# Orthogonal FFT convolution: the turned copy of U by a VectorE shuffle, and two copies moved from GpSimd to ScalarE

## The chip, the cores and the metric

The kernel runs on one core of a Trainium2 chip. The metric is the device time of one execution in microseconds, as the median over several executions. The profile is of one execution of its own.

## The reference, cut to what matters

```python
def cal_wfft_ortho(weight, n, cout, cin):            # n = 34, weight 128 x 127 x 3 x 3
    vfft = rfft2(weight, s=(n, n), norm='ortho')     # 34 x 18 frequencies
    vH = conj(swapaxes(vfft, -1, -2))
    wfft = vH @ vfft                                  # one 127 x 127 matrix per frequency
    eps = mean(diagonal(wfft)) * 1e-5
    wfft = wfft + eps * eye
    ortho = I - 2.0 * (vfft @ solve(wfft, vH))
    return ortho[:, :, :cout, :cin]

xfft = rfft2(pad(_gn(x)))                             # x: 32 x 128 x 32 x 32, group norm first
zfft = cal_wfft_ortho(weight, ...) @ xfft             # per frequency
out  = x + crop(irfft2(zfft)) + bias
```

Everything is fp32. For each of 580 frequencies (the ones that symmetry leaves over) a complex Hermitian 128 x 128 matrix has to be inverted, and its inverse applied to 32 images.

## The kernel before, in words

**Layout.** Four frequencies form a quad; there are 145 quads. A complex matrix is cut into 64 x 64 blocks, of which each is held over the 128 partitions as four row blocks ("quadrants" of 32 partitions); a quadrant has 16 rows of real parts and then the same 16 rows of imaginary parts. The quads are in two groups: group 0 has 82 quads in three sets, group 1 has 63 quads in two sets.

**Jobs.** `ORDER` is a list of jobs that all engines walk in the same order. `form` and `pre` build matrices with TensorE products (L947 to L983), `mid` solves the coupling between the first and the second half of the matrix (`turn`, `solve_b`, `schur`, L1034 to L1067), `final` applies the inverse to the images (`turn_q`, `solve_z`, `sum_y`). Between them stand the 16 `sweep` jobs: sweep k of a group eliminates pivot block k from all resident matrices of the group. Eight sweeps are on group 0 (11 units each: eight of 8 quads and three of 6), eight on group 1 (8 units each).

**Factoring.** Before a sweep VectorE factors its pivot blocks: `take`, `eliminate`, `scale`, then `place` once for each set (L1319 to L1378). It does so while TensorE runs the `pre`, `mid` or `final` job that stands ahead of the sweep. The sweep's first product waits for `factored` of its first set; in the group 0 sweeps VectorE still has two sets to place by then, in those of group 1 one.

**A unit of a sweep.** TensorE: `apply` (L995), 32 products of 32 rows by 64 columns for a unit of 8 quads, gives U in bank 0. ScalarE copies U to `u_emb[..., 0, :]` (`copy_u`, L1174). TensorE: `turn_u` (L1004), one product of 128 x 128 by 512 columns with a constant, gives the turned U (real and imaginary rows exchanged, one with a changed sign) in bank 1. ScalarE copies that to `u_emb[..., 1, :]` (`copy_ju`, L1180). TensorE: `update` (L1016), 32 products of 32 rows. VectorE subtracts the result from the matrices in four instructions (`update`, L1386), which pass on `upd_copied` after the second and after the fourth. TensorE's `update` of the next unit waits for the first of these. A product is shown in the trace as two matmul records, so 32 products are "x64". On TensorE the order is: apply(u+1), update(u), turn_u(u+1). After its copies of unit u+1 ScalarE copies pivot pieces of unit u-1 for the next sweep (`gather`, L1159).

**GpSimd** copies the solved first block (`copy_p`, L880 and L881, in `mid`; `copy_q`, L888, in `final`) from `M` to where it serves as weights, resets pivot columns (L871), and issues the stores (L898, L905). SP issues the loads. The last `final` job has 63 quads and no VectorE work beside it; after it comes the inverse transform (from L1410 on), which the change leaves alone.

## Time and profile of the kernel before

| | |
|---|---|
| median of 3 runs | 3135.11 us (3126.38 to 3148.89) |
| the profiled execution, device time | 3139.82 us |
| its span | 3137.1 us |
| mean granted TensorE clock | 0.869 of full speed |
| TensorE busy (matmul) | 2606.8 us, 83% |
| VectorE busy | 2014.0 us, 64% |
| ScalarE busy | 1269.0 us, 40% |
| GpSimd busy | 742.2 us, 24% |

A group of instructions is named by its line, engine, operation and shapes; then come its busy time, the mean of one in ns, and the engine's idle time just before them with what ended it. The TensorE clock has two levels, 2.4 GHz (1.00) and 1.2 GHz (0.50); a stretch's granted clock is the mean over it. T0 below is the time at which a sweep's first product starts.

### The profile page before, as it was taken

The numbers are of one execution on the slowest core, as the hardware profiler recorded it, in microseconds if no ns is written. First come the engines' busy times: TensorE is split into PE (matmuls) and PEld (weight loads), VectorE is DVE, ScalarE is ACT, GpSimd is POOL, SyncE is SP. The second block draws the span as 40 slices with busy tenths as digits, with TensorE's granted clock in tenths as the row PEclk, the third lists the DMA queues.
The fourth block names the chain that finished last, engine by engine and source line by source line (L and its number), as shares of the span: only waits on it lengthen the run. The fifth ranks groups of instructions, "written<-read, shape, count | busy, mean of one in ns | idle before, by whom it ended". The sixth has DMA issues, their size and how long they took to land. (4 is left out here: it accounts for less than half of the span.)

```text
span 3137.1 us, 89161 instructions
## 1 busy us (share of the span) xinstructions
PE 2606.8 (83%) x38281; PEld 2133.8 (68%) x38281; DVE 2014.0 (64%) x3842; ACT 1269.0 (40%) x2963; POOL 742.2 (24%) x1307
## 2 busy tenths in 40 slices
PE   3994919889999888998886968778888879959999
PEld 3663915555666677877775747566676768859999
DVE  5453710779788787787778889697887782003333
ACT  0441402443534255555533534343454444632221
POOL 0340000312121042332431414031343242520000
PEclk7897969989999899999988989797988899976787
DMA  4348073314231064754733516060231232566662
GB/s 171 104 110 149 2 121 67 123 56 163 68 113 40 15 129 81 139 110 80 158 67 62 109 29 135 3 136 13 93 95 53 65 120 77 164 140 162 169 168 92
DMA packets 562599, 310.00 MB, mean 99 GB/s; under 512 B 484616, under 2 KB 495496, under 8 KB 561368
## 3 DMA queue, kind: packets, MB, share of 16 engines
q1 hardware_dynamic: 520896, 183.58, 28.5%
q0 software_dynamic: 41312, 120.73, 11.4%
q8 instruction: 304, 4.98, 0.7%
q14 instruction: 87, 0.71, 0.1%
HBM read 162.85 MB, written 141.30 MB: 97 GB/s over the span
## 5 line engine op out<-in xcount | busy, mean ns | idle before, releaser
L1386 DVE SCALAR_TENSOR_TENSOR arena<-arena,psum 128x512 f32<-128x512 f32 (+2 forms) x608 | 399.0, 719 | 280.2 <-PE psum L1016 279.9
L1349 DVE TENSOR_TENSOR arena<-arena 128x960 f32<-128x960 f32 (+24 forms) x480 | 420.2, 876 | 16.6
L1344 DVE TENSOR_TENSOR arena<-arena 128x960 f32<-128x960 f32 (+8 forms) x600 | 403.9, 723 | 8.3
L953 PE MATMUL psum<-arena 128*32 128x256 f32 (+1 forms) x2904 | 263.9, 430 | 90.9 <-DMA arena<-plain 73.9
L995 PEld LDWEIGHTS psum<-arena 32*32 32x32 f32 x9280 | 160.5, 118 | 256.9 <-issue 240.4
L871 POOL COPY arena<-arena 128x512 f32<-128x512 f32 (+2 forms) x160 | 87.1, 594 | 1040.0 <-ACT arena L1159 1040.0
L1016 PE MATMUL psum<-arena 32*128 32x64 f32 x9280 | 313.1, 282 | 9.8 <-ACT arena L1180 9.8
L1016 PEld LDWEIGHTS psum<-arena 32*128 32x128 f32 x9280 | 291.7, 197 | 34.5 <-ACT arena L1180 20.4
L995 PE MATMUL psum<-arena 32*32 32x64 f32 x9280 | 187.0, 235 | 135.9 <-DVEq L1378 125.7
L957 PE MATMUL psum<-arena 128*32 128x256 f32 (+1 forms) x3696 | 264.5, 373 | 0.0
L1159 ACT COPY arena<-arena 32x128 f32<-32x128 f32 (+3 forms) x496 | 222.2, 448 | 31.4 <-DVE arena L1386 12.5
L1062 PE MATMUL psum<-arena 128*128 128x160 f32 x1160 | 195.6, 311 | 17.6 <-ACT arena L1207 17.4
L1004 PE MATMUL psum<-arena 128*128 128x512 f32 (+2 forms) x304 | 186.1, 696 | 28.0 <-ACT arena L1174 26.3
L1180 ACT COPY arena<-psum 128x512 f32<-128x512 f32 (+2 forms) x152 | 87.2, 574 | 287.7 <-PE psum L1004 287.7
L953 PEld LDWEIGHTS psum<-arena 128*32 128x32 f32 x2904 | 100.3, 110 | 149.4 <-issue 79.6
L1062 PEld LDWEIGHTS psum<-arena 128*128 128x128 f32 x1160 | 168.5, 193 | 47.9 <-ACT arena L1207 44.3
L905 POOL DMA_DIRECT2D yhat<-arena x290 | 155.1, 540 | 192.1 <-ACT arena L1243 184.4
L957 PEld LDWEIGHTS psum<-arena 128*32 128x32 f32 x3696 | 135.2, 110 | 95.4 <-issue 40.8
L1491 PE MATMUL psum<-arena 68*128 68x64 f32 x1152 | 170.6, 321 | 30.1 <-DMA arena<-yhat 30.1
L1491 PEld LDWEIGHTS psum<-arena 68*128 68x128 f32 x1152 | 168.0, 236 | 30.4 <-issue 30.4
L1049 PE MATMUL psum<-arena 128*128 128x96 f32 x1160 | 159.0, 282 | 32.5 <-issue 24.9
L1049 PEld LDWEIGHTS psum<-arena 128*128 128x128 f32 x1160 | 152.2, 198 | 45.5 <-issue 43.7
(121 smaller groups left out, 4764.9 us busy)
## 6 DMA issues: line engine op xcount, KB each, us to landing
blocks<-arena POOLq DMA_DIRECT2D x145, 256.0 KB, 2.5
arena<-blocks SPq DMA_DIRECT2D x290, 128.0 KB, 2.8
kept<-arena POOLq DMA_DIRECT2D x145, 256.0 KB, 3.0
arena<-kept SPq DMA_DIRECT2D x145, 256.0 KB, 2.8
xhat<-arena SPq DMA_DIRECT2D x32, 580.0 KB, 13.0
arena<-xhat SPq DMA_DIRECT2D x580, 32.0 KB, 2.6
yhat<-arena POOLq DMA_DIRECT2D x290, 64.0 KB, 2.3
arena<-x SPq DMA_DIRECT2D x8, 2048.0 KB, 11.7
```

The lines of the kernel that those rows point to most:

```text
L953: pe.matmul(columns[quadrant(p)].rearrange("p (a k) n -> p a k n", k=m), K["ident"][:, quadrant(p)], spread(base[:, 0:m, :], 1, n), start= ...
L957: ins = pe.matmul(columns[quadrant(p), m * a:m * a + m, :], ccoef[:, FREQ[f0 + m * a][0], :], coefs[:, 0:m, L * p:L * p + L], start=False, ...
L995: ins = pe.matmul(psum[0][h, L * t:L * t + L], ce[h, sj % NCE, slot + t, :], M[h, home(q) + t, c, :], start=True, stop=True)
L1004: pe.matmul(psum[1][:, 0:L * n], K["nturn"], u_emb[:, u % 2, 0:n].rearrange("p t q r m -> p (t q) r m")[:, :, 0, :], start=True, stop=True ...
L1016: ins = pe.matmul(upd_bank(u, c)[:, L * t:L * t + L], rows.rearrange("p q r m -> p (q r m)"), real_half(rows), start=t == 0, stop=t == n - 1)
L1049: ins = pe.matmul(psum[2][:, 3 * NB * f:3 * NB * f + 3 * NB], emb[:, m % 2, 1, f].rearrange("p q r m -> p (q r m)"), bx[:, m % 3, f, :], s ...
L1062: pe.matmul(banks[:, f // 2, f % 2, :], emb[:, m % 2, 0, f].rearrange("p q r m -> p (q r m)"), work[:, m % 2, f, 0:5 * NB], start=f % 2 == ...
L1159: ins = act.copy(dt[h, t - GROUPS[g][0], :, slot:slot + n].rearrange("p m s -> p s m"), M[h, at:at + n, c, B * piv:B * piv + B])
L1344: ins = dve.tensor_tensor(pr, spread(R[:, t, :, :, j], 3, 2 * w_), both, ALU.mult)
L1349: link(dve.tensor_tensor(rest, rest, pr[:, :, h], op))
L1386: ins = dve.scalar_tensor_tensor(old, old, K["mask"][:, piv:piv + 1], upd_bank(u, c)[:, 0:L * n].rearrange("p (t n) -> p t n", n=L), ALU.m ...
L1491: ins = pe.matmul(S1[u % 2][:, i * 2 * H:(i + 1) * 2 * H], y_t[0:2 * N, q % 2, k, (b % BQ) * C:(b % BQ + 1) * C], i1[:, 0 if k < NK2 - 2 e ...
```

## The change

`turn_u` and `copy_ju` go. In their place VectorE runs `swap_u`, a `stream_shuffle` that exchanges the two groups of 16 partitions in each 32, from PSUM straight to `u_emb[..., 1, :]`. The sign that the product gave is put into the other copy: `copy_u` becomes an activation with a scale per partition (a new constant `sign`, -1 for real rows). U has two PSUM banks in turn, so `apply(u)` waits for the copies of unit u-2 instead of u-1. `update` waits for both copies. VectorE's `swap_u(u+1)` stands ahead of its `update(u)`; the first ones stand behind the `place` of a set. `copy_p` and `copy_q` move from GpSimd to ScalarE, with the same instructions. Lines of before are quoted without numbers of after.

```diff
-    if u:
-        pe.wait_ge(S["u_copied"], u)
+    if u >= 2:
+        pe.wait_ge(S["u_copied"], u - 1)
+        pe.wait_ge(S["u_swapped"], u - 1)
...
-    ins = pe.matmul(psum[0][h, L * t:L * t + L], ce[h, sj % NCE, slot + t, :],
+    ins = pe.matmul(psum[u % 2][h, L * t:L * t + L], ce[h, sj % NCE, slot + t, :],
...
-def turn_u(u):
-    q, n, p, sj = sweep_units[u]
-    pe.wait_ge(S["u_copied"], u + 1)
-    if u:
-        pe.wait_ge(S["ju_copied"], u)
-    pe.matmul(psum[1][:, 0:L * n], K["nturn"],
-              u_emb[:, u % 2, 0:n].rearrange("p t q r m -> p (t q) r m")[:, :, 0, :],
-              start=True, stop=True).then_inc(S["j_turned"], 1)
...
 def update(u):                                  # TensorE
-    pe.wait_ge(S["ju_copied"], u + 1)
+    pe.wait_ge(S["u_copied"], u + 1)
+    pe.wait_ge(S["u_swapped"], u + 1)
...
-    act.copy(u_emb[...][:, :, 0, :], psum[0][...]).then_inc(S["u_copied"], 1)
+    act.activation(u_emb[...][:, :, 0, :], psum[u % 2][...], ACT.Copy, scale=K["sign"]).then_inc(S["u_copied"], 1)
-def copy_ju(u): ...
...
+swap = [i + B if i < B else i - B for i in range(2 * B)]
+def swap_u(u):                                  # VectorE
+    q, n, p, sj = sweep_units[u]
+    dve.wait_ge(S["u_copied"], u + 1)
+    if u >= 2:
+        dve.wait_ge(S["upd_done"], u - 1)
+    dve.stream_shuffle(u_emb[:, u % 2, 0:n].rearrange("p t q r m -> p (t q) r m")[:, :, 1, :],
+                       psum[u % 2][:, 0:L * n].rearrange("p (a m) -> p a m", m=B), swap).then_inc(
+                           S["u_swapped"], 1)
...
 for t in range(n):
     place(set_job_at[g, k, GROUPS[g][t]], t)
+    if t:
+        swap_u(lo + t - 1)
 for u in range(lo, hi):
+    if lo + n - 1 <= u + 1 < hi:
+        swap_u(u + 1)
     update(u)
...
 elif kind == "mid":                             # ScalarE
     copy_b(lo)
+    copy_p(lo)
     copy_j(lo)
     for m in range(lo, hi):
         copy_t(m)
         if m + 1 < hi:
             copy_j(m + 1)
+            copy_p(m + 1)
         copy_s(m)
...
 # final, ScalarE: behind each copy_jq(m)
+    copy_q(m)
```

TensorE's queue at the start of the first sweep, before; L995 is `apply`, L1004 `turn_u`, L1016 `update`, and a name in brackets is the semaphore that the row waits for:

```order
L995 MATMUL psum<-arena 32x64 [waits v_factored,v_reset,v_pre_copied,v_form_copied]
L995 MATMUL psum<-arena 32x64 x31
L1004 MATMUL psum<-arena 128x512 [waits v_u_copied]
L995 MATMUL psum<-arena 32x64 [waits v_u_copied,v_reset,v_factored]
L995 MATMUL psum<-arena 32x64 x31
L1016 MATMUL psum<-arena 128x64 [waits v_ju_copied]
L1016 MATMUL psum<-arena 128x64 x31
L1004 MATMUL psum<-arena 128x512 [waits v_ju_copied,v_u_copied]
L995 MATMUL psum<-arena 32x64 [waits v_u_copied,v_reset,v_factored]
L995 MATMUL psum<-arena 32x64 x31
L1016 MATMUL psum<-arena 128x64 [waits v_upd_copied,v_ju_copied]
L1016 MATMUL psum<-arena 128x64 x31
```

The same place after the change, where `apply` stands at line 972 and `update` at 985:

```order
L972 MATMUL psum<-arena 32x64 [waits v_factored,v_reset,v_pre_copied,v_form_copied]
L972 MATMUL psum<-arena 32x64 x31
L972 MATMUL psum<-arena 32x64 [waits v_reset,v_factored]
L972 MATMUL psum<-arena 32x64 x31
L985 MATMUL psum<-arena 128x64 [waits v_u_swapped,v_u_copied]
L985 MATMUL psum<-arena 128x64 x31
L972 MATMUL psum<-arena 32x64 [waits v_u_copied,v_u_swapped,v_reset,v_factored]
L972 MATMUL psum<-arena 32x64 x31
L985 MATMUL psum<-arena 128x64 [waits v_upd_copied,v_u_swapped,v_u_copied]
L985 MATMUL psum<-arena 128x64 x31
```

The product with 512 columns is gone from every unit, and only products of 32 rows are left; the second `apply` waits for no copy.

VectorE's queue at the end of the placing of the first sweep, before; L1374 and L1377 are `place`, L1386 is `update`:

```order
L1374 SCALAR_TENSOR_TENSOR arena<-arena 128x16x16 [waits v_chain]
L1374 SCALAR_TENSOR_TENSOR arena<-arena 128x16x16
L1377 STREAM_TRANSPOSE arena<-arena 128x16x32 [waits v_chain]
L1386 SCALAR_TENSOR_TENSOR arena<-arena,psum 128x8x64 [waits v_chain,v_upd_done]
L1386 SCALAR_TENSOR_TENSOR arena<-arena,psum 128x8x64 x3
L1386 SCALAR_TENSOR_TENSOR arena<-arena,psum 128x8x64 [waits v_upd_done]
L1386 SCALAR_TENSOR_TENSOR arena<-arena,psum 128x8x64 x3
```

The same place after; L1352 and L1355 are `place`, L1365 is `swap_u`, L1375 `update` (L1386 before):

```order
L1352 SCALAR_TENSOR_TENSOR arena<-arena 128x16x16 [waits v_chain]
L1352 SCALAR_TENSOR_TENSOR arena<-arena 128x16x16
L1355 STREAM_TRANSPOSE arena<-arena 128x16x32 [waits v_chain]
L1365 STREAM_SHUFFLE arena<-psum 128x32x16 [waits v_chain,v_u_copied]
L1375 SCALAR_TENSOR_TENSOR arena<-arena,psum 128x8x64 [waits v_upd_done]
L1375 SCALAR_TENSOR_TENSOR arena<-arena,psum 128x8x64 x3
L1365 STREAM_SHUFFLE arena<-psum 128x32x16 [waits v_upd_done,v_u_copied]
L1375 SCALAR_TENSOR_TENSOR arena<-arena,psum 128x8x64 [waits v_upd_done]
L1375 SCALAR_TENSOR_TENSOR arena<-arena,psum 128x8x64 x3
```

Before, the L1386 rows followed one another with nothing between them; now one shuffle stands ahead of each four.

ScalarE's queue in the first `mid` job, before; L1207 is `copy_t`, L1199 `copy_j`, L1215 to L1217 `copy_s`, L1194 `copy_b`:

```order
L1207 COPY arena<-psum 128x4x96 [waits v_t_done]
L1199 COPY arena<-psum 128x32x16 [waits v_turned]
L1215 COPY arena<-psum 128x256 [waits v_s_done]
L1216 COPY arena<-psum 128x4x64
L1217 COPY arena<-psum 128x4x32
L1194 COPY arena<-arena 128x16x16 [waits v_s_done,v_bx_in2]
```

The same place after; L1182 is `copy_t`, L1174 `copy_j`, L1157 and L1158 `copy_p`, L1190 to L1192 `copy_s`, L1169 `copy_b`:

```order
L1182 COPY arena<-psum 128x4x96 [waits v_t_done]
L1174 COPY arena<-psum 128x32x16 [waits v_turned]
L1157 COPY arena<-arena 128x16x16 [waits v_s_done]
L1158 COPY arena<-arena 128x4x64
L1190 COPY arena<-psum 128x256 [waits v_s_done]
L1191 COPY arena<-psum 128x4x64
L1192 COPY arena<-psum 128x4x32
L1169 COPY arena<-arena 128x16x16 [waits v_s_done,v_bx_in2]
```

The two rows of `copy_p` are new there, between the copy of the turned blocks and the wait for `schur`; the other rows keep their order.

## Rows read from the trace of the kernel before

**Rows 1.** Waits of TensorE, whole span: us in total, times, longest

```profile
PE psum L995 <- DVEq L1378: 125.7, 10, 24.6
```

**Rows 2.** Timeline of a steady unit of a sweep, 2.4 GHz: start, us, instructions

```profile
671.66 1.13 PE L1004 MATMUL psum<-arena 128*128 128x512 f32 x2
671.80 2.72 DVE L1386 SCALAR_TENSOR_TENSOR arena<-arena,psum 128x512 f32<-128x512 f32 x4 [1.30 <-PE psum L1016]
...
672.72 1.09 PE L995 MATMUL psum<-arena 32*32 32x64 f32 x64
...
673.75 2.01 PE L1016 MATMUL psum<-arena 32*128 32x64 f32 x64
...
675.69 1.13 PE L1004 MATMUL psum<-arena 128*128 128x512 f32 x2
```

**Rows 3.** Stages (length, busy PE, PEld, DVE, ACT, POOL, clock, DMA, GB/s): group 0 sweeps

```profile
2126.70:2182.20 55.50, 51.91 (x1335) 39.56 (x1335) 37.35 (x57) 12.43 (x22) 1.06 (x2) 0.80 0.01 3
sum 416.30, PE 381.57 PEld 289.36 DVE 293.00 ACT 196.74 POOL 28.97; mean PE 47.70 PEld 36.17 DVE 36.63 ACT 24.59 POOL 3.62
```

**Rows 4.** Stages: the sum over the four group 1 sweeps behind `final` jobs

```profile
sum 165.40, PE 149.32 PEld 112.87 DVE 100.34 ACT 71.37 POOL 9.43; mean PE 37.33 PEld 28.22 DVE 25.09 ACT 17.84 POOL 2.36
```

**Rows 5.** Stages: the first of the four group 1 sweeps behind `mid` jobs

```profile
1190.30:1226.20 35.90, 31.97 (x1025) 24.54 (x1025) 21.51 (x32) 20.11 (x45) 2.96 (x5) 0.97 0.11 22
```

**Rows 6.** Timeline inside the sweep of rows 3, where the clock rises

```profile
2138.79 1.93 PE L995 MATMUL psum<-arena 32*32 32x64 f32 x64
...
2140.65 3.69 PE L1016 MATMUL psum<-arena 32*128 32x64 f32 x64
...
2144.27 2.08 PE L1004 MATMUL psum<-arena 128*128 128x512 f32 x2
...
2146.28 1.93 PE L995 MATMUL psum<-arena 32*32 32x64 f32 x64
...
2148.14 2.49 PE L1016 MATMUL psum<-arena 32*128 32x64 f32 x64
2150.56 1.13 PE L1004 MATMUL psum<-arena 128*128 128x512 f32 x2
```

**Rows 7.** Stages: 20 us inside the same sweep, ahead of the rise

```profile
2129.00:2149.00 20.00, 19.70 (x342) 14.45 (x346) 12.10 (x18) 3.80 (x7) 0.00 (x0) 0.50 0.01 2
```

**Rows 8.** Costliest groups, shapes apart: copies of the shapes that the change adds or is near to

```profile
L1243 ACT ACTIVATE arena<-psum,arena 128x256 f32<-128x256 f32 x145 | 68.2, 477 | 63.9 <-DMA yhat<-arena 34.0 <-PE psum L1096 29.8
L1215 ACT COPY arena<-psum 128x256 f32<-128x256 f32 x145 | 54.1, 373 | 193.9 <-PE psum L1066 193.9
L1231 ACT COPY arena<-arena 128x256 f32<-128x256 f32 x145 | 51.1, 402 | 0.1
L1539 DVE COPY arena<-psum 108x512 f32<-108x512 f32 x64 | 44.2, 690 | 194.5 <-PE psum L1506 194.5
```

**Rows 9.** Timeline of the start of the first sweep of group 0

```profile
646.67 1.93 PE L995 MATMUL psum<-arena 32*32 32x64 f32 x64 [5.17 <-DVEq L1378]
...
654.21 1.06 DVE L1377 STREAM_TRANSPOSE arena<-arena 128x512 f32<-128x512 f32 x1
...
655.71 2.72 DVE L1386 SCALAR_TENSOR_TENSOR arena<-arena,psum 128x512 f32<-128x512 f32 x4 [0.44 <-PE psum L1016]
```

**Rows 10.** Timeline of the start of the sweep of rows 5

```profile
1196.24 2.72 DVE L1386 SCALAR_TENSOR_TENSOR arena<-arena,psum 128x512 f32<-128x512 f32 x4 [11.50 <-PE psum L1016]
```

**Rows 11.** Stages: group 0 factoring to T0, sum of four beside `pre`, then beside `mid`

```profile
sum 329.90, PE 307.32 PEld 181.82 DVE 313.87 ACT 104.06 POOL 84.46; mean PE 76.83 PEld 45.45 DVE 78.47 ACT 26.02 POOL 21.11
...
sum 358.10, PE 241.87 PEld 216.58 DVE 342.14 ACT 142.34 POOL 131.06; mean PE 60.47 PEld 54.15 DVE 85.53 ACT 35.59 POOL 32.77
```

**Rows 12.** GpSimd's groups from 1600 to 2126 us (63 quads of `mid`)

```profile
L881 POOL COPY arena<-arena 128x256 f32<-128x256 f32 x63 | 46.4, 736 | 0.0
...
L880 POOL COPY arena<-arena 128x256 f32<-128x256 f32 x63 | 41.9, 666 | 35.1 <-DVE arena L1386 35.1
```

**Rows 13.** GpSimd's group from 2182 to 2582 us (82 quads of `final`)

```profile
L888 POOL COPY arena<-arena 128x256 f32<-128x256 f32 x82 | 50.6, 627 | 54.5 <-DVE arena L1386 54.5
```

More of the change, by code:

```diff
@@ L77 @@
 CONST_AT, CONST_W = {}, 0
-for _name, _w in [("ident", P), ("mask", LB), ("turn", P), ("nturn", P), ("eblock", B), ("unit", 2 * B), ("tri", B * B),
+for _name, _w in [("ident", P), ("mask", LB), ("sign", 1), ("turn", P), ("nturn", P), ("eblock", B), ("unit", 2 * B), ("tri", B * B),
                   ("reset", LB * B), ("avg", P), ("trace", P), ("tcoef", 2 * NTERM * NK2)]:
@@ L185, in tables @@
     c["mask"] = i[:, None] // (2 * B) != np.arange(LB)[None]
+    c["sign"] = np.where(ri == 0, -1.0, 1.0)[:, None]
     turn = np.zeros((P, P))
@@ L918, in _ @@
                         elif kind == "mid":
-                            pool.wait_ge(S["upd_copied"], 2 * before("sweep", at))
                             pool.wait_ge(S["formed"], before("form", at))
@@ L927, in _ @@
                             for m in range(lo, hi):
-                                copy_p(m)
-                                if m > lo:
-                                    store_part(m - 1)
-                            store_part(hi - 1)
+                                store_part(m)
                         elif kind == "final":
-                            pool.wait_ge(S["s_done"], before("mid", at))
-                            pool.wait_ge(S["upd_copied"], 2 * before("sweep", at))
-                            for m in range(lo, min(lo + 4, hi)):
-                                copy_q(m)
                             for m in range(lo, hi):
                                 store_y(m)
-                                if m + 4 < hi:
-                                    copy_q(m + 4)
                     for n in range(2):
@@ L1113, in _ @@
                             apply(lo)
-                            turn_u(lo)
                             for u in range(lo, hi):
@@ L1173, in copy_u @@
                             act.wait_ge(S["upd_done"], u - 1)
[L1174 to L1181 removed]
+                        act.activation(u_emb[:, u % 2, 0:n].rearrange("p t q r m -> p (t q) r m")[:, :, 0, :],
+                                       psum[u % 2][:, 0:L * n].rearrange("p (a m) -> p a m", m=B),
+                                       ACT.Copy, scale=K["sign"]).then_inc(S["u_copied"], 1)
                     def copy_blocks(m):
@@ L1188, in copy_blocks, with copy_p, copy_q @@
                                  psum[6 + m % 2].rearrange("p (b f n) -> p b f n", b=2, f=QUAD)).then_inc(S["pre_copied"], 1)
+                    def copy_p(m):
+                        if m >= 2:
+                            act.wait_ge(S["s_done"], m - 1)
+                        src = M[:, home(mid_quads[m]), :, :]
+                        dst = emb[:, m % 2, 1].rearrange("p f q r m -> p (f q) r m")[:, :, 0, :]
+                        act.copy(dst, src.rearrange("p f n -> p (f n)").rearrange("p (a b) -> p a b", b=B))
+                        act.copy(work[:, m % 2, :, 0:L], src).then_inc(S["p_copied"], 1)
+                    def copy_q(m):
+                        src = M[:, home(final_quads[m]), :, :].rearrange("p f n -> p (f n)").rearrange("p (a b) -> p a b", b=B)
+                        dst = q_emb[:, m % 4].rearrange("p f q r m -> p (f q) r m")[:, :, 0, :]
+                        act.copy(dst, src).then_inc(S["q_copied"], 1)
                     def copy_b(m):
@@ L1279, in _ @@
                             act.wait_ge(S["formed"], before("form", at))
-                            act.wait_ge(S["upd_done"], before("sweep", at))
+                            act.wait_ge(S["upd_copied"], 2 * before("sweep", at))
                             copy_b(lo)
+                            copy_p(lo)
                             copy_j(lo)
@@ L1294, in _ @@
                             pairs = [range(m, min(m + 2, hi)) for m in range(lo, hi, 2)]
+                            act.wait_ge(S["upd_copied"], 2 * before("sweep", at))
                             for m in pairs[0]:
                                 copy_jq(m)
+                                copy_q(m)
                             for n, two in enumerate(pairs):
@@ L1303, in _ @@
                                     copy_jq(m)
+                                    copy_q(m)
                                 for m in two:
@@ L1402, in _ @@
                         scale(n)
+                        lo, hi = [job[3:5] for job in jobs if job[0:3] == ("sweep", g, k)][0]
                         for t in range(n):
                             place(set_job_at[g, k, GROUPS[g][t]], t)
-                        for u in range(*[job[3:5] for job in jobs if job[0:3] == ("sweep", g, k)][0]):
+                            if t:
+                                swap_u(lo + t - 1)
+                        for u in range(lo, hi):
+                            if lo + n - 1 <= u + 1 < hi:
+                                swap_u(u + 1)
                             update(u)
```

30 lines of the change are left out of this document (3 added, 27 removed).

## Prediction

> **What bounds the kernel now.** I read the timeline around each kind of job, then the stages with their clock, then the waits. The main part is a chain of stages on TensorE, and TensorE is nearly always busy in it. Its one long wait is for VectorE's factoring: 125.7 us, at the start of ten sweeps [rows 1]. So there are two kinds of time to look at: the units of the 16 sweeps, which TensorE bounds, and the factorings, which VectorE bounds where the TensorE job beside them is shorter.
>
> In a steady unit at 2.4 GHz TensorE goes without a gap from one turn product to the next: 675.69 - 671.66 = 4.03 us, of which the turn takes 672.72 - 671.66 = 1.06, `apply` 1.03 and `update` 1.94. VectorE works 2.72 us of it and waits 1.30 [rows 2].
>
> Not all sweeps run at this clock. In the sweep of rows 3 the granted clock is 0.80; the first 20 us behind its start are at 0.50, that is 1.2 GHz [rows 3, 7]. There a unit is 2148.14 - 2140.65 = 7.49 us: `apply` 1.86, `update` 3.62, turn 2.01. Then the clock rises: the `update` at 2148.14 takes 2.49 instead of 3.69, and the next turn 1.13 instead of 2.08 [rows 6]. What TensorE had done just before was a turn product (2144.27) and an `apply` (2146.28). This matters for the change, since it takes every turn product away. In the 20 us of rows 7 TensorE was busy for 19.70 us and the clock stayed at 1.2 GHz all the same, so being busy with this mix was not enough by itself; and of the mix the turn was the only product over all 128 rows.
>
> **The change, part by part.**
>
> (a) **A unit at 2.4 GHz.** VectorE gets a shuffle of 128x512 from PSUM. No row shows one. Bounds: 0.69 us, a VectorE copy of 512 elements from PSUM [rows 8], and 1.06, its transpose of 128x512 [rows 9]. It passes data straight through like the copy, in runs of 16, so I take 0.75. VectorE then needs 2.72 + 0.06 (its last instruction's tail) + 0.08 (two waits already met) + 0.75 = 3.61. TensorE's chain is: the first half of VectorE's update (half of 2.72 and the same 0.06, 1.42), 0.05 to pass it on, and from `update`'s start to VectorE's next 2.08 (673.75 to 671.80 + 4.03) [rows 2]; 3.55 together. The unit is thus about 3.6 instead of 4.03, and 3.92 with a shuffle of 1.06. ScalarE's copy of U gets a scale; a scaled copy of 256 elements takes 0.477 where a plain one takes 0.373 [rows 8], so 0.60 becomes 0.70, in the shadow of VectorE's update except at a sweep's start.
>
> The Trainium skill, page "VectorE: DVE Perf Modes", section on the perf-mode tier table, has STREAM_SHUFFLE at one element per cycle and about 2400 ns for 2048 elements; a quarter of that, 0.60 us and some fixed cost, would be an estimate near the lower bound. No run here shows it yet.
>
> (b) **A unit at 1.2 GHz.** TensorE bounds it: 1.86 + 3.62 = 5.48 us [rows 6]. A unit of 6 quads has three quarters of the products, 4.11. The question is whether the clock rises during such a sweep. I take it that it does not. Of the 16 sweeps, the 12 that start behind a wait for VectorE start at 1.2 GHz (the first `apply` of rows 9 takes 1.93 us where one at 2.4 GHz takes 1.09 [rows 2]), and in the last of group 0 the clock was down for more than two whole units, turn products and all, before it rose [rows 3, 6, 7]. Without the turn, what is left per microsecond is the same 32-row products at the same low rate. Besides, TensorE gets a new gap in the group 0 sweeps: its `update` of the second unit needs the first half of VectorE's first update, which comes about 11.5 us after T0 (below), while at 2.4 GHz its own work would end at 8.
>
> (c) **Group 0 sweeps (8).** Two shuffles stand in VectorE's placing. Placing ended at 655.27, 8.6 us after T0 [rows 9]; with two shuffles the first update starts at 10.1 instead of 9.04. TensorE's second `update` then starts at 11.6 and, at 1.2 GHz, VectorE's second update at 11.6 + 3.69 [rows 6] + 0.07 = 15.3. Six more units of 5.48: 48.2. Three of 4.11: 60.5. The last update takes 2.2: 62.7 us. Eight make 502, against 416.3 [rows 3]: **+85**.
>
> (d) **Group 1 sweeps behind `final` (4).** They start at 1.2 GHz too. The first swap ends 4.9 after T0 (one placing of 4.1, then the shuffle), `update` 3.76 more, VectorE's first update at 8.7; seven units of 5.48 less the last one's eighth: 46.4, then 2.4: 48.6. Four make 194, against 165.4 [rows 4]: **+29**.
>
> (e) **Group 1 sweeps behind `mid` (4).** TensorE comes straight from dense work, the clock is 0.97 [rows 5], and the new mix keeps TensorE busy for 2.97 of 3.6 us. I take it to stay up. The start shortens: the first update came 5.9 after T0 [rows 5, 10]; now 1.15 + 0.70 + 0.05 + 0.75 + 0.05 + 2.08 = 4.8. Seven units save 0.43 each: 4.2 in all, of which I count 3.5, since phases may slip. **-14**.
>
> (f) **Factoring without GpSimd's copies.** The same group 0 factoring takes VectorE 313.9 us in four stages beside `pre` and 342.1 beside `mid`; the stages are 329.9 and 358.1 long [rows 11]. Beside `mid` GpSimd copies for 46.4 + 41.9 = 88.3 us [rows 12]; beside `pre` it only issues stores. I put the 28.2 us down to these copies (0.32 us per us of copying). These stages end with a wait for VectorE, so most of it comes back: **-27**. In `final` the copies are 50.6 us [rows 13], worth 16 at most and 0 at least, since in the timeline TensorE's own work ends only a few us ahead of VectorE's there; I take **-10**. Beside the first four `mid` jobs TensorE is the longer one: nothing.
>
> (g) **ScalarE's new copies.** In `mid` two copies of about 0.40 (as L1231) stand where ScalarE waits for `schur`: 193.9 us over 145 quads, 1.34 each [rows 8]. 0.80 fits, at no cost. Without that cover it would be 0.80 on each of the 82 quads of TensorE-bound `mid` jobs, 66 us. In `final` 0.40 per quad mostly takes waiting time for stores that have to land (34.0 us before L1243 [rows 8]); the start of each `final` job loses about 0.5 us since four GpSimd copies no longer run ahead, and the last job some 2. The first `mid` gains 1. **+3**.
>
> **Sum.** 85 + 29 - 14 - 27 - 10 + 3 = **+66 us** on the profiled execution's 3139.8, which is 3206. That execution was 4.7 above the median of 3135.1, so for a median: **3200 us**, 2% slower.
>
> **The rivals.**
>
> *The clock recovers in the sweeps as before.* For it: it did so in every one of them before. Then (c) is +1.1 at the start, -0.43 x 7 and about -0.6 x 3 on the smaller units, -3.7 each, and some 8 more over the eight for their 1.2 GHz units that lack a turn: -38; (d) is about -4.5 each and 4 more: -22; with (e) -14, (f) -37, (g) +3 that is -108: 3027 us. With the shuffle at its upper bound 40 less is gained, 3067. This is the one on the other side. It decides by a single thing: whether TensorE gets back to 2.4 GHz within the first two or three units without a turn product. If it does so late, or only in some sweeps, the time lies between: each group 0 sweep that wakes is worth 15 us, and half of them would give about 3130. The Trainium skill, page "TensorE: Matmul & The Clock Gate", section "What's actually happening", says that the throttled state is the default and activity releases it. By that rule a TensorE that is always busy would come back, and the rival's 3027 would be the time; the trace agrees only in part, for rows 7 show 19.70 of 20 us busy at 0.50.
>
> *The clock is lost in the other sweeps too.* The four of (e) would take 48 instead of 32.5: +62, 3262 us. It needs them to start at 1.2 GHz or fall to it; against it are the 0.97 and their dense predecessor.
>
> *The factoring is not relieved.* If its 28 us come from something else than GpSimd's copies (the load traffic beside `mid`, for one), (f) is gone: 3237.
>
> *ScalarE becomes late in `mid`.* +66, 3266. Against it the 1.34 us.
>
> **How the numbers follow.** Likeliest, clock stays down in the 12 sweeps: 0.70, in which its own range is 3150 to 3250 (the relief gone at one end, two or three sweeps that wake at the other). Clock recovers in all: 0.14. In some: 0.10. Lost in the other four too, or ScalarE late: 0.06. The range that holds the time 8 times in 10 is 3090 to 3265. A change of 1%, 31 us, is about what a measurement of this kernel can tell. Below 3104: 0.17; within 3104 to 3166: 0.15; above: 0.68.
>
> **What would show it.** The product with 512 columns gone from the sweeps, and 152 shuffles of 0.7 to 0.8 us. Granted clock near 0.50 over whole group 0 sweeps of about 62 us, with `update` starts 5.5 apart; near 1.0 in the four sweeps behind `mid`, about 32 us long. Group 0 factoring beside `mid` at some 82.5 us to T0 like beside `pre`. ScalarE's wait before `copy_s` down from 1.34 to about 0.5, with `mid` jobs as long as before. Wrong it is if a group 0 sweep is back at 2.4 GHz by its third or fourth unit; then the time is near 3027.

## The result and the profile of the changed kernel

The changed kernel takes 3233.32 us (median of 4 runs, 3226.89 to 3236.53), the kernel before 3142.0 in the same comparison (3126.38 to 3153.34). The ratio is 1.029, with a 95% interval of 1.024 to 1.034: slower, as predicted, 33 us above the predicted 3200 and inside the range. All ratios below are to the kernel before, timed in the same comparison, with their 95% interval in brackets.

| | before | after |
|---|---|---|
| span of the profiled execution | 3137.1 us | 3225.1 us |
| mean granted TensorE clock | 0.869 | 0.783 |
| TensorE busy | 2606.8 us | 2705.2 us |
| VectorE busy | 2014.0 us | 2047.0 us |
| ScalarE busy | 1269.0 us | 1337.9 us |
| GpSimd busy | 742.2 us | 507.6 us |

TensorE is 98 us longer busy although 304 matmul records fewer stand there. The stages say where. First the eight group 0 sweeps of the changed kernel (columns as in [rows 3]; one of the eight, then the sum over all):

```profile
2189.90:2254.00 64.10, 56.73 (x1313) 53.48 (x1313) 45.19 (x79) 7.59 (x11) 1.06 (x2) 0.50 0.01 3
sum 507.50, PE 449.26 PEld 423.39 DVE 356.29 ACT 164.68 POOL 32.28; mean PE 56.16 PEld 52.92 DVE 44.54 ACT 20.58 POOL 4.03
```

This sweep lasts 64.10 us at a clock of 0.50, where [rows 3] has 55.50 at 0.80. The third number from the end is the granted clock: in these 64 us 2.4 GHz was not granted at all. Five of the eight sweeps show 0.50, three 0.53.

Next the four group 1 sweeps behind `mid` jobs, and the sum over the four:

```profile
1229.10:1275.30 46.20, 40.02 (x1008) 37.67 (x1008) 27.80 (x48) 17.14 (x36) 3.05 (x5) 0.57 0.09 17
1362.90:1396.30 33.40, 25.44 (x1009) 23.17 (x1009) 27.90 (x48) 17.29 (x37) 3.11 (x5) 0.95 0.14 25
1477.80:1521.00 43.20, 35.68 (x1009) 33.08 (x1009) 28.00 (x48) 17.23 (x37) 3.05 (x5) 0.66 0.10 19
1607.30:1664.10 56.80, 41.67 (x1009) 39.46 (x1009) 27.75 (x49) 16.64 (x20) 7.08 (x13) 0.54 0.09 15
sum 179.60, PE 142.80 PEld 133.38 DVE 111.45 ACT 68.30 POOL 16.30; mean PE 35.70 PEld 33.34 DVE 27.86 ACT 17.08 POOL 4.07
```

One of the four stayed at 2.4 GHz up to its last product (0.95), and it is the only sweep of the sixteen that became shorter: 33.40 us against 36.5. The other three fell to 1.2 GHz. Two of them did so at their start; the one at 1477.80 only 14 us later, at 1491.8, hence its 0.66.

Last, the four group 0 factorings beside `mid`, up to the sweep's first product, and the groups of the new instructions (mean of one in ns behind the busy time):

```profile
sum 331.10, PE 239.68 PEld 216.87 DVE 315.13 ACT 180.68 POOL 53.78; mean PE 59.92 PEld 54.22 DVE 78.78 ACT 45.17 POOL 13.45
```

```profile
L1365 DVE STREAM_SHUFFLE arena<-psum 128x512 f32<-128x512 f32 x120 | 102.5, 856 | 0.2
L1141 ACT ACTIVATE arena<-psum,arena 128x512 f32<-128x512 f32 x120 | 86.4, 721 | 434.9 <-PE psum L972 434.8
L1190 ACT COPY arena<-psum 128x256 f32<-128x256 f32 x145 | 54.0, 372 | 112.3 <-PE psum L1035 112.3
```

The second sum of [rows 11], 358.10 with VectorE 342.14, has become 331.10 with 315.13. ScalarE's wait ahead of `copy_s`, 193.9 in [rows 8], is 112.3.

The whole difference of the spans, 88.0 us, by stage:

| stages | before | after | moved | predicted |
|---|---|---|---|---|
| group 0 sweeps (8) | 416.3 | 507.5 | +91.2 | +85 |
| group 1 sweeps behind `mid` (4) | 156.7 | 179.6 | +22.9 | -14 |
| group 1 sweeps behind `final` (4) | 165.4 | 186.3 | +20.9 | +29 |
| group 0 factoring to T0 beside `mid` (4) | 358.1 | 331.1 | -27.0 | -27 |
| first four `mid` jobs | 347.3 | 336.6 | -10.7 | 0 |
| first four `final` jobs | 276.3 | 269.9 | -6.4 | -10 |
| the rest (work ahead of the first sweep, the `pre` jobs, last `final`, inverse transform) | | | -2.9 | 0 |
| ScalarE's copies, spread | | | (in the rows above) | +3 |

Each stage time is of one execution. How far such a sum moves by itself can be seen below: the run `e3_copies_only` has the sweeps of the kernel before, and its eight group 0 sweeps took 423.5 us where the kernel before took 416.3. So a few us in a row of this table show nothing.

### The profile page after: what moved, and what is told of

Same layout as the page of the kernel before. It is cut to its first block and busy times, and to the rows that moved or that the text cites. A ratio compares the mean times of both kernels' runs of the same rounds, so it can differ in the third digit from the quotient of the medians.

```text
span 3225.1 us, 88844 instructions
## 1 busy us (share of the span) xinstructions
PE 2705.2 (84%) x37977; PEld 2372.0 (74%) x37977; DVE 2047.0 (63%) x4146; ACT 1337.9 (41%) x3246; POOL 507.6 (16%) x872
## 5 line engine op out<-in xcount | busy, mean ns | idle before, releaser
L985 PE MATMUL psum<-arena 32*128 32x64 f32 x9280 | 508.7, 401 | 70.5 <-DVE arena L1375 39.0
L1375 DVE SCALAR_TENSOR_TENSOR arena<-arena,psum 128x512 f32<-128x512 f32 (+2 forms) x608 | 398.7, 718 | 254.7 <-PE psum L985 254.1
L985 PEld LDWEIGHTS psum<-arena 32*128 32x128 f32 x9280 | 482.7, 308 | 97.0 <-issue 62.1
L1327 DVE TENSOR_TENSOR arena<-arena 128x960 f32<-128x960 f32 (+24 forms) x480 | 399.7, 833 | 16.6
L1322 DVE TENSOR_TENSOR arena<-arena 128x960 f32<-128x960 f32 (+8 forms) x600 | 383.2, 688 | 8.2
L972 PE MATMUL psum<-arena 32*32 32x64 f32 x9280 | 262.4, 295 | 118.1 <-DVEq L1356 85.0
L972 PEld LDWEIGHTS psum<-arena 32*32 32x32 f32 x9280 | 229.8, 158 | 138.1 <-issue 124.7
L1141 ACT ACTIVATE arena<-psum,arena 128x512 f32<-128x512 f32 (+2 forms) x152 | 106.3, 700 | 521.8 <-PE psum L972 521.8
L933 PE MATMUL psum<-arena 128*32 128x256 f32 (+1 forms) x3696 | 269.9, 372 | 0.0
L929 PEld LDWEIGHTS psum<-arena 128*32 128x32 f32 x2904 | 110.5, 110 | 141.4 <-issue 80.2
L933 PEld LDWEIGHTS psum<-arena 128*32 128x32 f32 x3696 | 145.9, 110 | 83.8 <-issue 37.7
L884 POOL DMA_DIRECT2D kept<-arena x145 | 103.0, 710 | 521.0 <-ACT arena L1192 492.9
L1533 DVE COPY arena<-psum 108x512 f32<-108x512 f32 (+1 forms) x96 | 57.4, 598 | 195.1 <-PE psum L1500 194.3
```

Source lines behind the costliest of these rows:

```text
L929: pe.matmul(columns[quadrant(p)].rearrange("p (a k) n -> p a k n", k=m), K["ident"][:, quadrant(p)], spread(base[:, 0:m, :], 1, n), start= ...
L933: ins = pe.matmul(columns[quadrant(p), m * a:m * a + m, :], ccoef[:, FREQ[f0 + m * a][0], :], coefs[:, 0:m, L * p:L * p + L], start=False, ...
L972: ins = pe.matmul(psum[u % 2][h, L * t:L * t + L], ce[h, sj % NCE, slot + t, :], M[h, home(q) + t, c, :], start=True, stop=True)
L985: ins = pe.matmul(upd_bank(u, c)[:, L * t:L * t + L], rows.rearrange("p q r m -> p (q r m)"), real_half(rows), start=t == 0, stop=t == n - 1)
L1322: ins = dve.tensor_tensor(pr, spread(R[:, t, :, :, j], 3, 2 * w_), both, ALU.mult)
L1327: link(dve.tensor_tensor(rest, rest, pr[:, :, h], op))
```

## The experiments

Two questions stood open. Does the loss come from the shuffle's stages alone, with the copies a gain of their own (what the prediction says), or do the two depend on each other? And is the loss truly the clock, held down by what the products are, or by how much of the time TensorE works? The second has a plain test: give TensorE back a product that nobody uses, once over all 128 rows and once over 32, and change nothing else. Such a filler writes into the bank that `apply` overwrites just after it, so nothing of what is computed changes.

### The copies alone, and the shuffle alone

First the kernel before with `copy_p` and `copy_q` moved, and nothing else:

```diff
 # ScalarE, kernel before
+    copy_p(lo)                     # mid; copy_p(m + 1) and final's copy_q(m) as in the change
 # GpSimd
-    copy_p(m)
-    copy_q(m)
```

> The kernel before with only copy_p and copy_q moved from GpSimd to ScalarE; turn product kept. Theory (GpSimd's copies slow VectorE's factoring beside mid and final, ScalarE has room): group 0 factoring beside mid falls from 99 to 92 us, four stages lose 27 us together, the mid stages of group 0 some 10 and final some 6: about 3098. Rival (the relief seen after comes from the lower clock or load traffic): 3142, unchanged. Rival (ScalarE late): above 3142.

It took 3105.58 us (3092.61 to 3111.46), a ratio of 0.988 (0.985 to 0.992). Its four group 0 factorings beside `mid`:

```profile
sum 330.50, PE 240.37 PEld 216.78 DVE 314.47 ACT 179.03 POOL 53.72; mean PE 60.09 PEld 54.19 DVE 78.62 ACT 44.76 POOL 13.43
```

Then the changed kernel with these copies back on GpSimd:

```diff
 # GpSimd, changed kernel
+    copy_p(m)
+    copy_q(m)
 # ScalarE
-    copy_p(m)
-    copy_q(m)
```

> The kernel after with copy_p and copy_q back on GpSimd; the shuffle and the sign in ScalarE's copy kept. If the two parts of the change add up: 3233 + 44 = about 3277, sweeps as after (63.4 us for group 0), factoring beside mid as before (99 us). If ScalarE's extra copies had cost something in the kernel after, less than 3270.

It took 3289.18 us (3268.04 to 3296.39), 1.046 (1.041 to 1.051). The same four stages:

```profile
sum 359.40, PE 243.44 PEld 217.72 DVE 343.40 ACT 144.54 POOL 136.00; mean PE 60.86 PEld 54.43 DVE 85.85 ACT 36.14 POOL 34.00
```

330.50 without the copies on GpSimd and 359.40 with them, whichever way the turned U is made: the relief of the factoring is due to the copies and to nothing else in the change. The two parts nearly multiply (0.988 x 1.046 = 1.033 against 1.029). With the shuffle alone all four sweeps behind `mid` lost the clock (194.9 us in all), with both, three did. That need not be the copies' doing: it is one sweep of one execution.

How a copy slows VectorE can be read in the timeline of the kernel before (start, us, instructions), VectorE and GpSimd in one stretch:

```profile
2082.19 1.03 DVE L1336 SCALAR_TENSOR_TENSOR arena<-arena 128x27 f32<-128x27 f32 x1
...
2088.42 0.18 DVE L1336 SCALAR_TENSOR_TENSOR arena<-arena 128x24 f32<-128x24 f32 x1
```

```profile
2082.36 0.48 POOL L880 COPY arena<-arena 128x256 f32<-128x256 f32 x1
2082.70 0.48 POOL L881 COPY arena<-arena 128x256 f32<-128x256 f32 x1
```

An instruction of 27 elements took 1.03 us and ended at 2083.22, when GpSimd's two copies were over (2083.18); its sister, with no copy beside it, took 0.18. That looks like waiting for the copies, and not like running slowly beside them. It is one instruction, read as an example. The Trainium skill, page "SBUF — State Buffer", section "Who interferes with whom", says that VectorE and GpSimd share one pair of ports and that the lock on it is exclusive; these rows agree with it.

### A filler over 128 rows, and one over 32

The changed kernel with the old turn product's shape ahead of each `apply`, on constants, with no one waiting for it:

```diff
+    pe.matmul(psum[u % 2][:, 0:512], K["nturn"], consts[:, 0:512], start=True, stop=True)
     for t in range(n):             # apply(u)
```

> The kernel after, plus one product of 128 rows by 512 columns of constants ahead of every apply, whose result the apply overwrites, so nobody waits for it. It only takes TensorE time (about 1.06 us at 2.4 GHz, 2.0 at 1.2). Clock theory (sweeps are slow because without the turn product TensorE stays at 1.2 GHz): the granted clock comes back after two or three units as in the kernel before; a unit is 1.06 + 1.03 + 1.94 = 4.03 us again, group 0 sweeps near 51 us instead of 63.4, the whole near 3100 to 3120, although TensorE has 152 products more to do. Rival (the shuffle in VectorE's chain and its waits made the sweeps slow): TensorE gets more work and nothing is given back, group 0 sweeps of 63 us or, with 2.0 more per unit, up to 85; the whole 3233 to 3480.

It took 3106.18 us (3091.37 to 3130.92), 0.990 (0.984 to 0.996). One group 0 sweep, and the sum over all eight:

```profile
2105.80:2157.30 51.50, 46.28 (x1334) 34.44 (x1334) 45.73 (x79) 7.61 (x11) 1.04 (x2) 0.90 0.01 3
sum 412.30, PE 369.01 PEld 275.28 DVE 360.30 ACT 164.26 POOL 32.35; mean PE 46.13 PEld 34.41 DVE 45.04 ACT 20.53 POOL 4.04
```

TensorE has more products to do, and is done 12.6 us earlier than in the sweep of the changed kernel shown above. All sixteen sweeps were at 2.4 GHz for most of their length (clock 0.76 in the one with the long wait for a gather, 0.89 or more in the others), and the span is shorter by 3225.1 - 3099.8 = 125.3 us.

The same filler over 32 rows, with as many columns:

```diff
+    pe.matmul(psum[u % 2][:, 0:512], K["nturn"][0:32, :], consts[0:32, 0:512], start=True, stop=True)
```

> As the run with the full filler, but the filler has 32 rows instead of 128, the same 512 columns and so about the same time on TensorE. If what gives the clock back is that TensorE is kept busy without gaps, this does it as well as the full filler: about 3110. If it must be a product over all 128 rows, the sweeps stay at 1.2 GHz and each unit gets about 2.0 us longer, 7.5 instead of 5.5: group 0 sweeps near 83 us, the whole near 3480 to 3540.

It took 3467.79 us (3431.56 to 3479.46), 1.100 (1.092 to 1.109), the slowest of all and a little under the 3480 of the second expectation. One group 0 sweep and the sum over the eight, all of them at 0.50:

```profile
806.60:887.20 80.60, 76.92 (x1338) 58.17 (x1341) 45.30 (x78) 23.58 (x52) 4.80 (x8) 0.50 0.01 2
sum 643.50, PE 614.27 PEld 464.20 DVE 362.41 ACT 164.81 POOL 32.21; mean PE 76.78 PEld 58.02 DVE 45.30 ACT 20.60 POOL 4.03
```

This pair decides the second question for the group 0 sweeps. In the row of 806.60 TensorE is busy for 76.92 of 80.60 us, 95%, and stays at 1.2 GHz throughout; with the same number of products and columns over all 128 rows the clock is 0.90 and the sweep 51.50 us. Both units fill TensorE; they differ in the rows that the filler covers, and at 1.2 GHz the fillers take alike (2.02 and 2.08 us). The Trainium skill, page "TensorE: Matmul & The Clock Gate", section "What's actually happening", has activity release the throttle. By that rule alone the thin filler should have done as well as the full one; the two runs contradict it where activity is read as being busy. Other numbers of rows were not tried, so the runs show this for 32 and 128 rows only.

The thin filler says something on losing the clock too. One of its four sweeps behind `mid` stayed at 2.4 GHz (38.2 us, clock 0.91). The other three started at 2.4 GHz and were at 1.2 about 2 us later (60.9, 60.5 and 67.5 us, clock 0.51 or 0.52), with no idle time of TensorE between their start and the fall.

### Is the filler needed all along?

The prediction has the mix of `apply` and `update` hold 2.4 GHz, but not raise the clock. Then two fillers at the start of a sweep should do, where nothing lowers the clock afterwards.

```diff
+    if u - first < 2:              # `first` is the sweep's first unit
+        pe.matmul(psum[u % 2][:, 0:512], K["nturn"], consts[:, 0:512], start=True, stop=True)
```

> The kernel after with the filler of 128 rows by 512 columns only ahead of the first two applys of each sweep. Theory: the new mix can hold 2.4 GHz but not raise it, and the three group 1 sweeps behind mid that lost it lost it at their start. So the sweeps behind mid stay at 2.4 GHz at least twice more often than in the kernel after, near 36 us where they hold it; group 0 sweeps and those behind final start at 1.2 GHz, have a gap of some 3 us behind the first update, and stay at 1.2 for the rest, 63 to 67 and 47 to 50 us. Whole 3205 to 3240. Rival (the filler is needed only to start): all sweeps come back to 2.4 GHz, near 3080.

It took 3197.35 us (3185.14 to 3209.02), 1.019 (1.013 to 1.024), a little under the range expected. The group 0 sweeps stayed slow, 504.5 us together. The four group 1 sweeps behind `final` did not: 148.6 us together. One of them:

```profile
2426.90:2463.70 36.80, 29.03 (x1012) 25.09 (x1012) 31.33 (x53) 17.30 (x36) 3.31 (x6) 0.87 0.03 8
```

The group 0 part of the expectation held, and the part on the sweeps behind `final`, which did not, is the more telling. TensorE's timeline at the start of the last group 0 sweep (L971 is the filler, L976 `apply`, L989 `update`):

```profile
2195.49 2.05 PE L971 MATMUL psum<-arena 128*128 128x512 f32 x2 [18.21 <-DVEq L1360]
2197.47 1.93 PE L976 MATMUL psum<-arena 32*32 32x64 f32 x64
2199.33 2.08 PE L971 MATMUL psum<-arena 128*128 128x512 f32 x2
2201.34 1.10 PE L976 MATMUL psum<-arena 32*32 32x64 f32 x64
2202.37 2.01 PE L989 MATMUL psum<-arena 32*128 32x64 f32 x64
...
2208.01 3.59 PE L989 MATMUL psum<-arena 32*128 32x64 f32 x64 [2.54 <-DVE arena L1379]
```

The two fillers raise the clock: the `apply` at 2201.34 takes 1.10, the `update` 2.01. Then TensorE waits 2.54 us for VectorE, which is still placing the third set, and the next `update` is back at 3.59. Nothing raises the clock again in the 50 us that follow. All eight group 0 sweeps have such a wait, of 2.54 to 3.36 us, and in all eight the clock is back at 1.2 GHz before the `update` behind it is over. Behind `final` jobs the sweep has one set less to place, so this wait is missing:

```profile
2436.14 2.01 PE L989 MATMUL psum<-arena 32*128 32x64 f32 x64 [0.59 <-DVE arena L1379]
...
2439.77 2.01 PE L989 MATMUL psum<-arena 32*128 32x64 f32 x64 [0.58 <-DVE arena L1379]
```

Here the same mix, with no filler, keeps 2.4 GHz up to the last `update`, through a wait of 0.58 to 0.69 us in each unit, and all four sweeps take 36.7 to 37.8 us. I had expected 47 to 50, by which two fillers would not have been enough there. The last `update` stands behind a wait of 1.61 us and takes 3.26 to 3.40. So the mix can hold the clock through waits of about 0.6 us, and in this run waits of 1.6 to 3.4 us stood ahead of a fall. That is a reading of what stood where: no run changed one wait alone.

It is not the whole story either. Of the four sweeps behind `mid`, two kept the clock (36.8 us each, as expected), one met its long wait for a gather (56.9), and the one at 1238.10 lost it near 1252.5, in its steady units (44.2 us). TensorE had no wait for another engine there. It had paused for 0.77 and 0.78 us within the two `apply` before, pauses for which the trace names nothing; in the two sweeps that kept the clock such pauses were of up to 1.00 us.

### How little filler will do

A filler of half the columns ahead of every `apply`:

```diff
+    pe.matmul(psum[u % 2][:, 0:256], K["nturn"], consts[:, 0:256], start=True, stop=True)
```

> The kernel after with a filler of 128 rows by 256 columns of constants ahead of every apply (half of that in e1_full_filler; result overwritten by the apply). Clock theory: it still raises the clock in the group 0 sweeps, within a few units, and at 2.4 GHz it takes about 0.53 us, so TensorE needs 0.53 + 1.03 + 1.94 = 3.50 us per unit and VectorE's 2.72 + 0.86 + 0.06 = 3.64 bounds it instead of the 4.03 with the full filler: 0.39 less on some 150 units, less what the later rise costs: 3055 to 3085, against 3106. If half a product is too little to raise the clock, TensorE's unit at 1.2 GHz is 6.5 us, group 0 sweeps 73 us, the whole near 3340.

3105.64 us is the median of two executions near 3083 and two near 3129 (3081.74 to 3130.52), a ratio of 0.986 (0.977 to 0.995): above what was expected, and not clearly better than the full filler. The profile is of the slowest execution. Two group 0 sweeps of it:

```profile
1700.00:1749.20 49.20, 41.75 (x1335) 35.01 (x1335) 44.35 (x78) 23.69 (x52) 4.80 (x8) 0.92 0.02 3
2130.40:2202.60 72.20, 64.38 (x1334) 54.70 (x1334) 45.79 (x79) 7.58 (x11) 0.99 (x2) 0.57 0.01 2
```

The same instructions took 49.2 us with the clock at 0.92 and 72.2 at 0.57. In the second the clock rose for some 10 us at the start and then stayed down; whether that tells the slower executions from the faster ones is open, since none of the faster was profiled. With 512 columns in a sweep's first four units and 128 in the others:

```diff
+    w = 512 if u - first < 4 else 128
+    pe.matmul(psum[u % 2][:, 0:w], K["nturn"], consts[:, 0:w], start=True, stop=True)
```

> The kernel after with a filler of 128 rows, 512 columns ahead of the first four applys of each sweep and 128 columns ahead of the others. Theory: the first four raise the clock as in e1_full_filler, the mix with a short filler then holds it, and VectorE bounds the later units at 3.64 to 3.7 us: group 0 sweeps near 49 us, the whole 3060 to 3090. If the mix does not hold the clock behind a stall, single sweeps fall back to 1.2 GHz and show 55 us or more.

3095.85 us (3080.51 to 3126.61), 0.986 (0.979 to 0.993). It was expected at 3060 to 3090. Six group 0 sweeps took 48.2 to 49.6 us, but two 60.9 and 68.9. What tells the good from the bad sweeps, with the same instructions, was not found. Last, 512 columns in the first six units and 256 in the others:

```diff
+    w = 512 if u - first < 6 else 256
+    pe.matmul(psum[u % 2][:, 0:w], K["nturn"], consts[:, 0:w], start=True, stop=True)
```

> The kernel after with a filler of 128 rows: 512 columns ahead of the first six applys of a sweep, 256 ahead of the others. In e8_graded_filler the clock rose within the first four units in most sweeps but not in all (two group 0 sweeps of 61 and 69 us), and in e6_half_filler 256 columns everywhere raised it late. Theory: six long fillers raise it in every sweep, 256 columns hold it and stay below VectorE's 3.64 us per unit. Group 0 sweeps 49 to 52 us, group 1 sweeps 36 to 39, the whole 3075 to 3095. If the rise depends on something else than the long fillers, single group 0 sweeps above 58 us remain and the whole stays at 3095 to 3110.

```profile
2086.90:2135.80 48.90, 43.26 (x1335) 33.56 (x1335) 45.32 (x79) 7.59 (x11) 1.00 (x2) 0.92 0.02 4
sum 392.70, PE 348.47 PEld 270.44 DVE 357.21 ACT 163.13 POOL 31.65; mean PE 43.56 PEld 33.80 DVE 44.65 ACT 20.39 POOL 3.96
```

3069.64 us (median of 6, 3065.22 to 3083.48) against 3141.59 of the kernel before, a ratio of 0.979 (0.974 to 0.983). All eight group 0 sweeps took 48.6 to 50.3 us. This is the shuffle's gain, got at last: 392.7 us in these sweeps against 416.3 before and 507.5 in the changed kernel, and the fastest version of this study, somewhat under the 3075 to 3095 expected. Of its 2.1% the moved copies alone are 1.2 (the run with the copies alone), so shuffle and fillers together bring the rest.

## Why the prediction was right, and where it was wrong

**(a) The unit at 2.4 GHz: right.** The shuffle takes 0.856 us, inside the bounds (0.69 to 1.06) and above the 0.75 taken. In the one sweep that kept its clock VectorE's updates start at 1367.88 and 1371.50, 3.62 apart, where 3.6 was predicted and [rows 2] has 4.03. The scaled copy takes 0.721 (0.70 predicted).

**(b) The unit at 1.2 GHz: right, its reason nearly.** TensorE in the last group 0 sweep of the changed kernel:

```profile
2211.54 1.93 PE L972 MATMUL psum<-arena 32*32 32x64 f32 x64
...
2213.40 3.69 PE L985 MATMUL psum<-arena 32*128 32x64 f32 x64
...
2217.02 1.93 PE L972 MATMUL psum<-arena 32*32 32x64 f32 x64
```

2217.02 - 2211.54 = 5.48 us, as worked out from [rows 6]. That the clock stays down was the choice on which the forecast rested, and all eight group 0 sweeps spent their steady units at 1.2 GHz. The two fillers bear out the reason, that without the products over all rows the mix did not raise it. But the sweep at 1894.03 shows an exception that the prediction did not have:

```profile
1894.03 3.64 PE L972 MATMUL psum<-arena 32*32 32x64 f32 x128 [19.75 <-DVEq L1356]
1899.17 2.01 PE L985 MATMUL psum<-arena 32*128 32x64 f32 x64 [1.50 <-ACT arena L1141]
1901.12 1.69 PE L972 MATMUL psum<-arena 32*32 32x64 f32 x64
```

Behind two `apply` in a row, products of 32 rows only, the `update` runs at 2.4 GHz, and the next `apply` is on its way back to 1.2. That happened in three of the eight (hence their 0.53) and in two of the sweeps behind `final`, and lasted for no more than 4 us each time; in the other five of the eight the same two `apply` did not do it. So the clock can rise behind narrow products too; `apply` and `update` in turn never raised it.

**(c) Group 0 sweeps: +91.2 for +85.** The sum was short at the start. The second `update` starts at 2202.44, 12.5 us after T0 at 2189.94, not 11.6:

```profile
2189.94 3.63 PE L972 MATMUL psum<-arena 32*32 32x64 f32 x128 [20.15 <-DVEq L1356]
...
2200.91 2.70 DVE L1375 SCALAR_TENSOR_TENSOR arena<-arena,psum 128x512 f32<-128x512 f32 x4
...
2202.44 3.69 PE L985 MATMUL psum<-arena 32*128 32x64 f32 x64 [1.02 <-DVE arena L1375]
```

The `update` waits for VectorE there. VectorE's first update starts 11.0 us after T0, where 10.1 was worked out, right behind the second shuffle: the placing and two shuffles of 0.856 us, each with 0.23 us of idle time ahead, take longer than 8.6 + 2 x 0.75. TensorE's first `update` was over at 2199.5 and is not what it waits for. That makes 0.9 us in each sweep, 7 in all, where 6 are missing from the sum.

**(d) Group 1 sweeps behind `final`: +20.9 for +29, direction right, premise half right.** The sum itself has a slip: 46.4 + 2.4 is 48.8, not 48.6, which is 1 us over the four. "They start at 1.2 GHz too" holds for two of the four. (Already in the kernel before it did not hold for all of the twelve: the sweep at 2465.60 begins with an `apply` of 1.09 us, and of the twelve only ten wait for VectorE, as [rows 1] says.) The other two start at 2.4 GHz and lose it in the first unit. The second of them:

```profile
2435.55 2.00 PE L972 MATMUL psum<-arena 32*32 32x64 f32 x128 [2.30 <-issue]
2438.42 2.01 PE L985 MATMUL psum<-arena 32*128 32x64 f32 x64 [0.88 <-ACT arena L1141]
2440.36 1.63 PE L972 MATMUL psum<-arena 32*32 32x64 f32 x64
```

Two `apply` and an `update` at 2.4 GHz make these sweeps shorter than worked out: 44.9 to 47.7 us instead of 48.6.

**(e) Group 1 sweeps behind `mid`: the step that failed.** +22.9 for -14, 37 us and thus the whole miss. The prediction says of the clock: "I take it to stay up", because TensorE comes from dense work and the new mix keeps it busy for 2.97 of 3.6 us. It stayed up in one of the four. Here are the starts of a sweep that lost the clock at once and of the one that kept it:

```profile
1229.07 2.00 PE L972 MATMUL psum<-arena 32*32 32x64 f32 x128 [1.17 <-issue]
...
1231.94 0.66 PE L985 MATMUL psum<-arena 32*128 32x64 f32 x13 [0.87 <-ACT arena L1141]
1233.62 1.77 PE L985 MATMUL psum<-arena 32*128 32x64 f32 x51 [1.03 <-issue]
...
1235.33 1.51 PE L972 MATMUL psum<-arena 32*32 32x64 f32 x64
```

```profile
1362.94 2.00 PE L972 MATMUL psum<-arena 32*32 32x64 f32 x128 [1.17 <-issue]
...
1365.81 2.01 PE L985 MATMUL psum<-arena 32*128 32x64 f32 x64 [0.88 <-ACT arena L1141]
1367.75 1.10 PE L972 MATMUL psum<-arena 32*32 32x64 f32 x64
```

Both wait 1.17 us, work for 2.00 and wait 0.87 for the first copy and shuffle, a wait that the turn product used to fill. The first then stands for 1.03 us more, in which the trace shows nothing that TensorE waits for, within 64 records of one `update`, and the next `apply` is already on its way down (1.51 for 1.10). It is tempting to put the loss down to that pause. The trace of the run with the shuffle alone speaks against it; there `apply` is L997 and `update` L1010:

```profile
1368.60 2.00 PE L997 MATMUL psum<-arena 32*32 32x64 f32 x128 [1.17 <-issue]
1371.47 2.01 PE L1010 MATMUL psum<-arena 32*128 32x64 f32 x64 [0.87 <-ACT arena L1166]
1373.41 1.61 PE L997 MATMUL psum<-arena 32*32 32x64 f32 x64
```

This start is the same as that of the sweep that kept the clock, wait for wait, and this sweep lost it (44.9 us, clock 0.56). And with the thin filler, which fills the waits inside the start, three of four lost it still sooner. So idle time inside the start is not needed for the loss.

Nor is the steady unit safe. The sweep at 1477.80 has a pause of 1.84 us in its first two `apply`, goes on at 2.4 GHz all the same, and falls at 1491.8, in its fifth `apply`:

```profile
1485.45 2.01 PE L985 MATMUL psum<-arena 32*128 32x64 f32 x64 [0.16 <-DVE arena L1375]
...
1489.27 0.31 PE L972 MATMUL psum<-arena 32*32 32x64 f32 x7 [0.85 <-issue]
...
1493.58 3.69 PE L985 MATMUL psum<-arena 32*128 32x64 f32 x64
```

The fourth, at 1607.30, waits 10.94 us behind its `apply` for a gather and goes on at 1.2 GHz (`update` 3.69); it had a wait of that kind before the change as well (10.7 us) and came back to 2.4 GHz within 5 us of it, with turn products in the mix. The prediction took the one row of [rows 5] for all four.

What the runs show in place of the step is this: without the turn product the mix keeps 2.4 GHz in some sweeps and loses it in others, at the start or later, and once it is down the rest of the sweep stays at 1.2 GHz, but for the few us named in (b). What decides whether it falls stays open. With the full filler the four sweeps behind `mid` take 164.7 us in all, and only the one with the long wait for a gather is below 0.92.

The prediction had this as a rival, at no more than 0.06 and +62 us for the four; it came true in three, for 26 us together. The evidence named against it, the clock of 0.97 in [rows 5], is a row of a sweep that still had its turn products, and says nothing on a mix without them. That the time came out inside the range all the same is partly luck: the jobs of `mid` and the sweeps behind `final` came out shorter than worked out, by 11 and 8 us.

What makes the pauses stays open too. In the steady units of the sweeps at 1362.90 and 1477.80 they come 126 or 127 matmul records apart, or twice that, and an instruction transfer lies between 1231.2 and 1231.4, ahead of the pause of 1.03 us; that the supply of instructions came late is a guess from this order in time. It wasn't tried.

**(f) Factoring without GpSimd's copies: right to the microsecond beside `mid`**, -27.0 for -27, and now with its cause shown by two runs that moved nothing but these copies. In `final` it was -6.4 for -10, between the bounds 0 and -16, but no further from nothing than such a sum moves by itself.

**Not foreseen: -10.7 in the first four `mid` jobs.** The prediction has them bound by TensorE and so counts nothing. TensorE's busy time in them is the same (312.6 and 313.4 us), so its waits fell. With the copies alone these jobs take 340.2 us, 7 less than before, and with the shuffle alone 344.8; the larger part seems to come from the copies there too. In the second of them, waits of TensorE for ScalarE and of the kind the trace gives no reason for, 8.3 us of 89.4, became 5.7 of 87.6; I did not follow it further.

**(g) ScalarE's new copies: right.** The wait ahead of `copy_s` fell from 1.34 to 112.3 / 145 = 0.77 us a quad, and no job became longer for it. It fell less than the 0.80 of the two copies, so part of them lies elsewhere.

**The rivals.** *The clock recovers as before*: in no group 0 sweep did it last, but the price was sound: with fillers that do bring the clock back the time is 3069.64, near its 3067 with the slower shuffle, though TensorE then has the fillers to do; that the two numbers are so near is chance. *The factoring is not relieved* and *ScalarE becomes late in `mid`* are out by (f) and (g).

## What to carry to other kernels

A product on TensorE may be worth more than its result. Before one is moved to an idle engine, look in the timeline for what stood ahead of each rise of the granted clock; where it is the one product over all rows, and the rest is narrow, its removal can cost more than it saves wherever a stage starts behind a wait: here a unit of 5.48 us at 1.2 GHz instead of 4.03 at 2.4. And don't forecast the clock of a new mix from the old mix's row, nor from one good sweep: here one sweep of four held 2.4 GHz, and two with the same start, wait for wait, went different ways.

## What the runs showed of the hardware beyond what I expected

- TensorE can be busy for 76.92 of 80.60 us with 32-row products and be granted 1.2 GHz in all of it; 128-row fillers in the same places brought 2.4 GHz back about 6 us into the sweep at 2105.80.
- Behind two `apply` in a row, 3.45 to 3.64 us of 32-row products, 2.4 GHz came for about one `update` in five sweeps, and did not in five others; the alternation of `apply` and `update` never brought it in some 50 us.
- Two sweeps with the same start, `apply` 2.00 us, a wait of 0.87 or 0.88 and `update` 2.01, went on at 2.4 GHz in one run and at 1.2 in another.
- The same instructions bring the clock back at different times within one execution: 49.2 and 72.2 us for two group 0 sweeps with the half filler, 48.2 and 68.9 with 512 and then 128 columns.
- A shuffle of 128x512 fp32 from PSUM takes 856 ns, a quarter more than the copy of 690 in [rows 8]; the load of its mask, which goes with each, takes 14 ns.

- A copy on GpSimd cost VectorE's fp32 factoring about a third of its own length (28 us for 88.3 us of copies, [rows 11, 12]), in the row shown by what looks like holding an instruction until the copies were over.
